# Folded value matrices applied to the input once, windows by DMA, probabilities summed over heads in PSUM

## The reference, cut to what matters

```python
for i in range(6):
    x = attn_layer(shift_tokens(x), Wqkv[i], ...) + x   # 16 heads of 64, windows of 32
    x = ffn_layer(shift_tokens(x), ...) + x             # layer norm, 341 hidden, gelu gate
# attn_layer: q, k l2-normalised, rotated; each window of 32 queries sees 64 keys
#             (its own 32 tokens and the 32 before)
sim = where(mask, -max, einsum('bhwie,bhwje->bhwij', bq, bk2) * 8)
out = einsum('bhwij,bhwje->bhwie', softmax(sim), bv2); return out @ Wo
# shift_tokens: the upper 64 columns of each token come from the token before
```

## Time and profile before

| | us |
|---|---|
| median of 3 runs | 2100.1 (2099.26 to 2106.28) |
| profiled execution | 2100.06 |
| its span, first to last instruction | 2098.2 |
| PE / DVE / POOL / ACT busy | 1924.6 / 1560.9 / 1324.6 / 1290.3 |
| starts of the first and the last mask matmul | 389.12 / 2045.45 |

### The profile page before, as it was taken

How to read it: one execution, slowest core, us unless ns; L and a number is a source line. 1 busy time by engine, 2 the same in 40 slices (tenths; PEclk the granted TensorE clock), 3 DMA queues, 4 the chain that set the end, 5 groups by cost and what they waited for, 6 DMA issues and landing times. The chain is left out here.

```text
span 2098.2 us, 65778 instructions
## 1 busy us (share of the span) xinstructions
PE 1924.6 (92%) x27244; PEld 1523.1 (73%) x27244; DVE 1560.9 (74%) x2684; ACT 1290.3 (61%) x2082; POOL 1324.6 (63%) x1145
## 2 busy tenths in 40 slices
PE   6888886699999999999999999999999999999996
PEld 4665665577777777777777777777777877787774
DVE  4766865777887778877777877788776878787773
ACT  5666765356566656665656666657665666566654
POOL 2332343677786667776667866588666777676760
PEclk9999998899999999999999999999998999999999
DMA  3000001000000010000010000100000100000000
GB/s 99 2 0 0 0 1 57 15 3 2 2 2 2 2 55 2 2 3 2 2 55 2 2 2 2 55 3 2 2 2 6 52 2 2 2 3 6 2 7 16
DMA packets 12434, 25.12 MB, mean 12 GB/s; under 512 B 1856, under 2 KB 9728, under 8 KB 10496
## 3 DMA queue, kind: packets, MB, share of 16 engines
q1 hardware_dynamic: 12160, 21.16, 2.9%
HBM read 20.11 MB, written 1.05 MB: 10 GB/s over the span
## 5 line engine op out<-in xcount | busy, mean ns | idle before, releaser
L1061 PE MATMUL banks<-arena 128*128 128x128 f32 (+4 forms) x6052 | 672.8, 311 | 60.0 <-ACT arena L689 16.8
L1061 PEld LDWEIGHTS banks<-arena 128*128 128x128 f32 (+3 forms) x6052 | 558.5, 176 | 169.8 <-issue 70.6
L902 DVE TENSOR_TENSOR arena<-banks,tabs 128x1024 f32<-128x1024 f32 x192 | 235.2, 1225 | 133.6 <-ACT arena L646 125.0
L449 POOL TENSOR_TENSOR arena<-arena 128x1024 f32<-128x1024 f32 x96 | 230.6, 2402 | 66.0 <-DVE arena L907 65.8
L479 POOL TENSOR_TENSOR small<-small 128x33 f32<-128x33 f32 x100 | 24.6, 246 | 350.2 <-ACT small L736 350.2
L675 ACT ACTIVATE arena<-banks 128x1024 f32<-128x1024 f32 x96 | 98.7, 1028 | 238.2 <-PE banks L1218 238.2
L444 POOL TENSOR_TENSOR prob<-prob,small 128x1024 f32<-128x1024 f32 x96 | 182.7, 1903 | 82.9 <-DVE small L942 82.9
L907 DVE TENSOR_TENSOR arena<-banks,tabs 128x1024 f32<-128x1024 f32 x192 | 233.3, 1215 | 0.2 <-issue 0.2
L454 POOL TENSOR_TENSOR arena<-arena 128x1024 f32<-128x1024 f32 x96 | 228.7, 2382 | 4.0 <-DVE arena L907 4.0
L1218 PEld LDWEIGHTS banks<-cst,arena 128*128 128x128 f32 x1536 | 182.1, 142 | 28.9 <-issue 2.9
L1218 PE MATMUL banks<-cst,arena 128*128 128x128 f32 x1536 | 201.3, 275 | 1.0 <-ACT arena L675 1.0
(11 more groups left out here) (132 smaller groups left out, 3993.1 us busy)
## 6 DMA issues: line engine op xcount, KB each, us to landing
qkraw<-in_wqk_dram SPq DMA_DIRECT2D x6, 1024.0 KB, 5.5
arena<-in_wvo_dram SPq DMA_DIRECT2D x6, 1024.0 KB, 7.1
W<-in_w_dram SPq DMA_DIRECT2D x6, 341.0 KB, 8.6
W<-in_w_dram SPq DMA_DIRECT2D x6, 192.0 KB, 2.3
res<-in_x_dram SPq DMA_DIRECT2D x4, 256.0 KB, 4.2
tabc<-in_tab_dram SPq DMA_DIRECT2D x1, 1024.0 KB, 6.2
out_dram<-res SPq DMA_DIRECT2D x4, 256.0 KB, 2.3
sca_s<-in_sca_dram SPq DMA_DIRECT2D x6, 128.0 KB, 3.4
```

Of the source, the lines that this page charges most:

```text
L449: pool.tensor_tensor(kc, kc, ks, ALU.add).then_inc(s["k_add"], 1)
L902: dve.tensor_tensor(heads(c), heads(two(0)), table(k % NT, kind), ALU.mult).then_inc(s[done], 1)
L1061: return pe.matmul(o, l, r, start=start, stop=stop)
```

## The change

The folded matrices are applied to the input first. Per tile PE multiplies the shifted input of 128 tokens (`xsH`, `xsL`) by all 16 heads' M at once (`values`), 1024 columns for the even and 1024 for the odd heads, in split form: M is kept as MH and ML, in the place of the long attention's gxH and gxL. ACT copies each half from banks 4 and 5 to `vs` (`copy_values`). SP then issues five DMAs for each half that place the token ranges -32..31, 0..63, 32..95 and 64..127 of the tile in four slots of `vw`, even heads on partitions 0 to 63 and odd on 64 to 127, as the transposed probabilities lie; the last 32 tokens go to the slot of the next tile's first window, which has two copies. `weigh` multiplies `ptile` (32 queries of a window as weights) by vw and sums over the eight head pairs in bank 7: the result has tokens on partitions. So the residual stream `Xt` has tokens on partitions, `ln_rows` uses a shift matrix in place of transposes, `down` gives tokens on partitions, with the bias b2 as a row of W2 and a row of ones in `gl[2]`, and `layer_columns` transposes it back for the next layer. W2 has two buffers, `seeds` moves to POOL, the norm inputs `rin` have two copies, W1's, Wq's, Wk's and M's splits are spread over steps, and the calls of all four loops are in a new order. STEPS is one more.

```diff
+        gl = [arena[:, 9472 + CH * j:9472 + CH * (j + 1)] for j in range(3)]
+        vs = arena[:, 11008:13056].rearrange("p (o n) -> p o n", o=2)
+        vw = arena[:, 13056:18176].rearrange("p (s n) -> p s n", s=5)
+        xf = arena[:, 18176:18688]
+        WVO = arena[:, 18688:20736].rearrange("p (z k n) -> p z k n", z=2, k=NP)
+
+        def slot(k, w):
+
+            return w + 1 if w else k % 2
...
+            for k in range(LAST_TILE + 1):
+                l, n = divmod(k, TILES)
+                if k > 0:
+                    sp.wait_ge(s["o_mm"], k)
+                for o in range(2):
+                    sp.wait_ge(s[f"v_cp{o}"], k + 1)
+                    c0 = 64 * o
+                    for to, rows_of, at in ((slice(c0 + WIN, c0 + 64), slice(0, WIN), slot(k, 0)), (slice(c0, c0 + 64), slice(0, 64), 2),
+                                            (slice(c0, c0 + 64), slice(WIN, 96), 3), (slice(c0, c0 + 64), slice(64, P), 4),
+                                            (slice(c0, c0 + WIN), slice(96, P), slot(k + 1, 0))):
+                        sp.dma_start(vw[to, at, :], vs[rows_of, o, :]).then_inc(vd_in[o], 16)
...
+                rotate_keys(G - 2)
+                seeds(G - 2)
+                next_query_weights(G - 2)
+                next_table(G - 3)
+                refine(G - 2)
+                scale_keys(G - 2)
+                lookback(G - 2)
+                shifted_lower(chunk_at(G, 16))
                 lower_columns(G - 7)
+                rotate_queries(G - 2)
+                next_key_weights(G - 1)
                 scale_queries(G - 2)
-                next_key_weights(G - 1)
-                rotate_keys(G - 1)
                 scale_probs(G - 3)
-                shifted_lower(chunk_at(G, 15))
-                refine(G - 1)
-                scale_keys(G - 1)
-                lookback(G - 1)
-                next_query_weights(G - 1)
-                rotate_queries(G - 1)
-                next_table(G - 1)
...
-                    after(act, "z_mm", 2 * k)
+                    after(act, "o_mm", k)
                     act.activation(ptile[:, :, :], two(2).rearrange("p (k t) -> p k t", k=NP), ACT.Copy).then_inc(s["pt_cp"], 1)
...
+            def copy_values(k, o):
+                act.wait_ge(s[f"v_mm{o}"], k + 1)
+                if k > 0:
+                    act.wait_ge(vd_in[o], VD * k)
+                act.activation(vs[:, o, :], two(V_BANK), ACT.Copy).then_inc(s[f"v_cp{o}"], 1)
...
+                act.activation(halves(MH, r), two(2).rearrange("p (o n) -> p o n", o=2), ACT.Copy).then_inc(s["M_H"], 1)
...
+                    act.activation(lns[:, k % 2, 64:D], bk(LN_BANK)[:, 0:64], ACT.Copy).then_inc(s["ln_cp"], 1)
+                    act.activation(lns[:, k % 2, 0:64], Xt[:, k % TILES, 0:64], ACT.Copy).then_inc(s["ln_cp"], 1)
+
+            def copy_layer(c):
+                if c is not None and c < (DEPTH - 1) * NC:
+                    act.wait_ge(s["xT_mm"], c + 1)
+                    act.wait_ge(s["xs_L"], 2 * (c + NC))
+                    act.activation(xf[:, :], bk(XT_BANK), ACT.Copy).then_inc(s["xT_cp"], 1)
...
             for G in range(STEPS):
-                next_w1(chunk_at(G, 13))
+                gelu(chunk_at(G, 10), 1)
+                copy_even(G - 2)
+                next_query_upper(G - 1)
+                square_queries(G - 1)
+                copy_queries_T(G - 2)
                 gelu(chunk_at(G, 10), 0)
-                gelu(chunk_at(G, 10), 1)
-                square_queries(G - 1)
-                copy_windows(G - 3)
+                copy_odd(G - 2)
+                next_w1_upper(chunk_at(G, 11))
+                copy_probs(G - 3)
                 gelu(chunk_at(G, 10), 2)
+                copy_rows(G - 4)
+                roots(G - 1)
+                shifted_upper(chunk_at(G, 15))
                 copy_columns(G - 6)
-                copy_queries_T(G - 2)
-                next_products(G - 4)
-                roots(G - 1)
-                shifted_upper(chunk_at(G, 14))
-                copy_probs(G - 3)
-                copy_rows(G - 4)
+                next_key_upper(G)
+                next_folded_lower(G - 2)
                 square_keys(G)
                 copy_keys(G - 1)
-                copy_lower(G - 3)
+                next_folded_upper(G - 2)
                 exponentials(G - 2)
-                copy_upper(G - 3)
+                copy_layer(chunk_at(G, 12))
...
+                    dve.scalar_tensor_tensor(lnx[:, :], lns[:, k % 2, :], ag[:, k % 2, 0:1],
+                                             rs[:, 4, 32:33].to_broadcast([P, D]), ALU.subtract, ALU.mult).then_inc(s["ln_x"], 1)
...
+                    dve.wait_ge(s["r_cl"], k + 3)
+                    dve.tensor_scalar(rin[:, k % 2, 32:33], ag[:, k % 2, 1:2], 1e-5, None, ALU.add).then_inc(s["ln_eps"], 1)
+
+            def folded_lower(l, r):
+                dve.wait_ge(s["M_H"], 2 * l + r + 1)
+                dve.tensor_tensor(halves(ML, r), two(2).rearrange("p (o n) -> p o n", o=2), halves(MH, r), ALU.subtract)                   .then_inc(s["M_L"], 1)
...
+                    dve.tensor_tensor(Xt[:, t:t + 4, :], bk(DN_BANK).rearrange("p (t d) -> p t d", t=4), Xt[:, t:t + 4, :], ALU.add)                       .then_inc(s["x_new"], 1)
+                    if c >= (DEPTH - 1) * NC:
+                        dve.wait_ge(s["x_new"], c + 1)
+                        dve.tensor_tensor(res[:, t:t + 4, :], Xt[:, t:t + 4, :], res[:, t:t + 4, :], ALU.add).then_inc(s["fin_add"], 1)
...
             for G in range(STEPS):
-                sine_queries(G - 2)
-                maxima(G - 3)
                 subtract(G - 3)
+                normalise_rows(G - 6)
                 cosine_keys(G - 1)
+                next_rest_upper(G - 3)
                 sine_keys(G - 1)
-                normalise_rows(G - 6)
-                moments(G - 5)
-                next_biases(chunk_at(G, 13))
-                residual(chunk_at(G, 13))
-                gated(chunk_at(G, 11), 1)
                 denominators(G - 3)
                 sum_keys(G - 1)
-                gated(chunk_at(G, 12), 2)
+                next_biases(chunk_at(G, 13))
                 gated(chunk_at(G, 11), 0)
+                gated(chunk_at(G, 11), 1)
                 sum_queries(G - 1)
-                seeds(G - 1)
+                residual(chunk_at(G, 12))
+                gated(chunk_at(G, 11), 2)
                 cosine_queries(G - 1)
-                attended(G - 4)
-                last_add(chunk_at(G, 15))
+                next_w1_lower(chunk_at(G, 13))
+                sine_queries(G - 1)
+                moments(G - 4)
+                maxima(G - 2)
+                next_rest_lower(G - 2)
+                attended(G - 3)
...
+            def values(k, o):
+
+                b, i = tile_at(k)
+                xH, xL = xsH[:, b, P * i:P * (i + 1)], xsL[:, b, P * i:P * (i + 1)]
+                pe.wait_ge(s["xs_L"], 2 * (k // 4) + 2)
+                pe.wait_ge(s["M_L"], 2 * (k // TILES) + 2)
+                claim(V_BANK, V_BANK + 1)
+                for h in range(2):
+                    c0 = HD * o + 512 * h
+                    mm(bk(V_BANK + h), xH, MH[:, c0:c0 + 512], True, False)
+                    mm(bk(V_BANK + h), xH, ML[:, c0:c0 + 512], False, False)
+                    ins = mm(bk(V_BANK + h), xL, MH[:, c0:c0 + 512], False, True)
+                ins.then_inc(s[f"v_mm{o}"], 1)
+                freed[V_BANK] = freed[V_BANK + 1] = (f"v_cp{o}", k + 1)
...
+            def weigh(k):
+
                 if is_tile(k):
                     pe.wait_ge(s["pt_cp"], k + 1)
-                    pe.wait_ge(s["xw_cp"], k + 1)
-                    weigh(k, 0)
-
-            def weigh_upper(k):
-                if is_tile(k):
-                    weigh(k, 1)
-
-            def fold(r):
-
-                for q in range(4):
-                    for o in range(2):
-                        ins = mm(bk(M_BANK)[:, 0:P], M[:, r, o, q, :], zT[:, o, :, 4 * r + q, :],
-                                 (r, q, o) == (0, 0, 0), (r, q, o) == (1, 3, 1))
-                return ins
+                    pe.wait_ge(vd_in[0], VD * (k + 1))
+                    pe.wait_ge(vd_in[1], VD * (k + 1))
+                    claim(PV_BANK)
+                    for j in range(NP):
+                        for w in range(NW):
+                            ins = pe.matmul(bk(PV_BANK)[WIN * w:WIN * (w + 1), 0:D], ptile[:, j, WIN * w:WIN * (w + 1)],
+                                            vw[:, slot(k, w), D * j:D * (j + 1)], start=j == 0, stop=j == NP - 1,
+                                            skip_group_check=True)
+                    ins.then_inc(s["o_mm"], 1)
+                    freed[PV_BANK] = ("x1", k + 1)
...
-                    b, i = tile_at(k)
+                    n = k % TILES
                     pe.wait_ge(s["x1"], k + 1)
-                    claim(6, 7)
-                    for z in range(2):
```

(56 more changed lines are left out.)

311 lines of the change are left out of this document (142 added, 169 removed).

## The result

The changed kernel takes 2258.61 us (median of 4 runs, 2243.29 to 2264.17) against 2099.76 (2099.26 to 2106.28) for the kernel before on the same chip: a ratio of 1.0741, 95% interval 1.0706 to 1.0777. The forecast was 2082, with a range from 1975 to 2165; the measured time lies above it. The profiled execution took 2256.91 us, its span is 2255.1.

The account below looks back on a forecast made before the run. PE bounds the old kernel; after the change a one-buffer DMA ring would: 5.7 + 11.3 = 17.0 us a step. 95 x 17.0 plus 25 for boundaries is 1640 against 1656; 2100.1 - 16 - 2 = 2082 us, range 1975 to 2165.

Parts of the forecast that it names:

- The ring: Local-attention step: weigh's end, SP's DMAs, ACT's odd copy, mask, scores, next weigh; period 17.0 us, deciding instead of PE.
- the work behind the even copy: ACT's queue: projection squares, transposed queries and probabilities wait too, but have about 1 us to spare.
- half the rate: SBUF-to-SBUF transfers: each touches at most half of the partitions, so 2.10 MB per tile takes 9.6 us.
- Rival 1: Tile's DMAs: full rate, landing in 6.8 us, PE decides, steps of 16.0 us, 1987 us; chance 0.25.
- scores 1.41, weigh 1.98: PE's matmuls within the step's period: 1.41 us for scores, 1.98 us for weigh's 64 instructions at 31 ns.
- the PE part: PE's share of the step's 17.0 us period, mask through weigh: 4.3 us.
- D = 11.3: Tile's ten DMAs, first issue to last landing: 9.6 us of data plus 1.7, so 11.3 us.
- the fixed part: Tile's DMAs: time beyond the data, from a 256 KB transfer landing 2.3 us after issue; 1.7 us.
- Rival 2: ACT's odd copy waiting for DMAs: a dearer period, 95 us per us, 2168 at 12.2 us; chance 0.25.
- PE's work per step: Local-attention stage: 5.4 us added, 6.7 removed, so 15.6 us per step in place of 16.9.
- the five boundaries: Steps between layers: 5 us extra each in place of 10, 25 us together, 25 us to both sides possible.
- The fill and the tail: Start and end of the stage: tail gives 3 us, fill of first tile's DMAs takes about 1; net 2.

Follow-up runs that it names:

- e1: The changed kernel with each of a tile's ten transfers moving only the first 128 of 1024 columns of its rows; 2020.72 us.
- e8: The changed kernel with the ten transfers issued even, odd in turn; 2535.72 us.
- e4: The changed kernel with a second buffer for the odd half of the values, keys' and queries' squares sharing one array; 2113.95 us.
- e2: The changed kernel with the same 2.10 MB per tile in four transfers of all 128 partitions instead of ten; 2027.21 us.
- e3: The kernel before plus ten transfers per tile that only SP waits for, weight loads moved behind the seventh tile's; 2188.52 us against 2089.88.
- e10: The changed kernel with ACT, not DMA, copying the two in-place blocks, behind the folded matrices' split; 2078.44 us, 0.9921 of the kernel before.

## Why the prediction was wrong

- **Right: which chain decides.** The ring through SP's issues, the landing of the odd half and ACT's copy sets the step. ACT waits for DMAs and the mask for ACT, as it said. e1 shows that taking its data away takes its time away, and e8 that lengthening its even part lengthens the kernel. One thing beside it was wrong: the prediction gave the work behind the even copy about 1 us to spare, and ACT waits for the even half in 60 of 63 tiles between 700 and 1900 us (129.9 us, see e4).
- **Right: half the rate.** 9.6 us of data were forecast and 10.1 measured; e2 and the two transfers that stay in place show that the partitions touched are the reason. Rival 1 falls.
- **Failed: the term "scores 1.41, weigh 1.98" of the ring's period,** taken from the earlier trace rows, one undisturbed step. Such a step is what 53 and 42 of 89 tiles do (1.48 and 1.99 us with the last matmul's end), but the sum had no term for the tiles in which PE stops for instructions, nor for the lower granted clock. With the stops the kernel before already has 1.74 for the scores, a mean that a row by groups would have shown. The changed kernel has 1.99 and 2.56 in the ring. With mask to scores (0.95 for 0.73) and scores to weigh (0.42 for about 0.2), the PE part is 1.5 us longer than forecast: 95 x 1.5 = 143 us.
- **Failed: the term D = 11.3.** It was 12.0 without ACT's start: the packets take 10.1 us for 9.6, and the fixed part, from the first issue to the first packet (1.2) and from the last packet to ACT (0.7), is 1.9 for 1.7. That is 0.7 us, 95 x 0.7 = 67 us. SP's issues came about 0.77 us apart and not 0.5 (7.76 for ten in the row above), but the packets, not the issues, filled the time. Rival 2 named this place and this price; at its D of 12.2 it gave 2168, still 90 below the result, since it kept the forecast's PE part.
- **Left out: the traffic's own price on PE.** The part on the DMAs had terms for issue, rate and landing, none for engines that wait for no data. No run shows that this mattered: e2 and e1 stop for instructions alike with 135 and 26 GB/s, and e3's 98.6 us hold 52.9 of a late load. 0.27 us per tile of scores and weigh, 25 us of the 143 above, come beyond e1 with the lower clock.
- **Of little weight.** PE's work per step was forecast at 15.6 us; busy time in the stage is 225.21/270 x 19.16 = 16.0, and 246.33/270 x 16.69 = 15.2 in e1. The step over each of the five boundaries takes 20.9 to 23.1 us, the others 19.05 on the mean, so they cost 11 us together where 25 were forecast. The fill and the tail gave 3.1 and 4.3 us, where 2 were forecast for both.

The two terms are 143 + 67 = 210 us. The mean of 19.16 us holds the boundaries, for which the forecast had 25 us more, and start and tail gave 7 us where 2 were forecast: 2082 + 210 - 25 - 5 = 2262, against 2258.6. What stays open: why PE stops for instructions so much more often in the new order (after 430 us 56 times over 0.3 us, 66 in e1 and 61 in e2, for 10 in the kernel before). The change puts weigh close behind the scores, 192 small matmul instructions in about 3.7 us, which is the likely reason; no run moved them apart. Open is also why plain steps of e10 stay at 17 us when PE has about 15.5 us of work.

## What to carry to other kernels

A ring with one buffer costs its latency in every step, so each of its terms must be a mean over many steps with the waits for instructions in it, not the cleanest step; an error of 0.1 us is multiplied by the number of tiles. SBUF-to-SBUF transfers onto 32 or 64 partitions ran at about half the rate of those over 128 (208 and 356 GB/s), so count the partitions touched, not the bytes alone, and try whether an engine can write the blocks that stay on their partitions. When a copy has to wait for the last reader of its target, put everything that others wait for ahead of it, and nothing that itself waits behind PE's next stage. An experiment that adds transfers to a queue must leave the loads of that queue where they were, or it measures the load that comes late; look at which steps grew before naming a cause.

## What the hardware showed unexpectedly

- PE's stops within trains of small matmuls are waits for its next 256 instructions: in every trace looked at (10 stops over 0.3 us after 430 us in the kernel before, 56 in the changed one, 66 in e1, 61 in e2) they lie at the same place modulo 256 and end 1.2 to 1.7 us after a 16 KB packet of instructions. Eight times the data did not make them more.
- SBUF-to-SBUF traffic at 121 GB/s that no engine waits for, with the DMA engines busy for 53% of the time, cost a PE-bound kernel 0.1 us in an ordinary step of 17 us. Its largest price, 52.9 of 88.5 us, came where a load stood behind it in the queue and engines waited for that.
- Transfers to the two halves of the partitions in turn reached 218 GB/s, one half after the other 208, and all partitions at once about 356 as a mean and 448 in the best slice.
- After a stop of 1.69 us within the scores the granted clock fell, to a mean of 0.57 between 923.0 and 926.4 us, and weigh took 3.56 us for its 64 instructions in place of 1.99.
